# A graph network's first softmax stage: edge attributes loaded into the row buffers, gathers that add to them, and eight slots of rows in place of four

## What is computed

```python
h = jnp.maximum(_layernorm(x, axis=-1), 0.0)
# layer 0, per edge (src, dst) and per feature
m = jax.nn.relu(h[src] + edge_attr_64) + EPS
gmax = jax.ops.segment_max(m, dst, num_segments=N)
ex = jnp.exp(m - gmax[dst])
den = jax.ops.segment_sum(ex, dst, num_segments=N)
a = ex / den[dst]
msg = jax.ops.segment_sum(m * a, dst, num_segments=N)
...
# layer 1: mean of h[src] over dst; layer 2: a hyperbolic attention;
# layer 3: a relational attention with the same kind of softmax over dst
```

## Time and profile before

| | |
|---|---|
| Time, median of 3 runs | 9775.68 us (9775.22 to 9775.8) |
| Profiled execution, span from first to last instruction | 11897.1 us |
| PE busy | 6205.5 us (52%) |
| DVE busy | 7097.6 us (60%) |
| ACT busy | 4900.8 us (41%) |
| POOL busy | 7035.0 us (59%) |
| Gathers (indirect DMAs) of the four edge stages | 1664, 1664, 1840, 1664 |

### The profile page before, as it was taken

The page is one execution under the profiler, slowest core; times in us unless marked ns, Lnnn a source line. Parts: engine busy times, 40 slices in busy tenths (PEclk is TensorE's granted clock), DMA queues, the critical chain, the costliest instruction groups (busy, mean ns, idle before and its releaser), DMA issues. The chain is left out here.

```text
span 11897.1 us, 122808 instructions
## 1 busy us (share of the span) xinstructions
PE 6205.5 (52%) x28151; PEld 5446.9 (46%) x28151; DVE 7097.6 (60%) x14671; ACT 4900.8 (41%) x10378; POOL 7035.0 (59%) x7381
## 2 busy tenths in 40 slices
PE   3444444434255555551366666666665555555552
PEld 2444444432255555551356666666664344444441
DVE  5666666666455555531655555555555577777775
ACT  4555555532155555550244444444444222222221
POOL 5666666654666666667055555555554666666665
PEclk7667676665577777775555555555556666666665
DMA  5444444443222222222133444444444444444442
GB/s 117 112 111 111 111 110 110 110 89 130 55 56 57 56 56 56 57 55 20 32 78 79 81 81 80 80 82 80 80 81 135 106 116 115 115 116 113 116 114 78
DMA packets 1475564, 1051.26 MB, mean 88 GB/s; under 512 B 1027429, under 2 KB 1192798, under 8 KB 1474097
## 3 DMA queue, kind: packets, MB, share of 16 engines
q0 software_dynamic: 235520, 312.13, 14.7%
q1 hardware_dynamic: 842054, 371.05, 13.2%
q10 hardware_dynamic: 397557, 363.20, 9.4%
HBM read 574.49 MB, written 471.02 MB: 88 GB/s over the span
## 5 line engine op out<-in xcount | busy, mean ns | idle before, releaser
L1223 POOL DMA_INDIRECT h_rows_d<-table,h_idx_d x1840 | 1755.3, 954 | 1292.5 <-PE h_ps_sum L1243 698.0
L616 POOL DMA_INDIRECT rows<-table,idx_all x1664 | 1569.9, 943 | 974.7 <-issue 460.9
L1006 POOL DMA_INDIRECT m_rows<-table,idx_all x1664 | 1570.8, 944 | 877.4 <-issue 454.6
L616 POOL DMA_INDIRECT rows<-table3s,idx_all x1664 | 1570.0, 943 | 855.0 <-issue 475.8
L1036 PE MATMUL m_ps_sort<-m_hot_high,m_hot_low 128*128 128x224 f32 x3328 | 1050.4, 495 | 950.4 <-issue 793.0
L1036 PEld LDWEIGHTS m_ps_sort<-m_hot_high,m_hot_low 128*128 128x128 f32 x3328 | 916.0, 281 | 1056.0 <-issue 911.3
L1243 PE MATMUL h_ps_sum<-h_rows_d,h_hot 128*128 128x65 f32 x3680 | 831.3, 417 | 605.1 <-DVE h_rows_d L1380 354.6
L1243 PEld LDWEIGHTS h_ps_sum<-h_rows_d,h_hot 128*128 128x128 f32 x3680 | 794.8, 328 | 689.6 <-issue 689.6
L863 ACT ACTIVATE ex<-ex 128x512 f32<-128x512 f32 x416 | 261.9, 630 | 2010.3 <-issue 1060.6
L1261 PE MATMUL h_ps_src<-h_near,h_hot_t 128*128 128x65 f32 x3680 | 837.8, 419 | 405.9 <-DMA h_near<-table 218.0
L1261 PEld LDWEIGHTS h_ps_src<-h_near,h_hot_t 128*128 128x128 f32 x3680 | 804.1, 331 | 433.4 <-issue 432.5
(11 more groups left out here) (441 smaller groups left out, 15639.0 us busy)
## 6 DMA issues: line engine op xcount, KB each, us to landing
scan<-out_e ACTq DMA_DIRECT2D x832, 256.0 KB
h_near<-table SPq DMA_DIRECT2D x1840, 32.5 KB
run_g<-h_run ACTq DMA_DIRECT2D x230, 260.0 KB
part_b<-part SPq DMA_DIRECT2D x832, 64.0 KB
max_b<-top ACTq DMA_DIRECT2D x416, 128.0 KB
scan<-m_out_e SPq DMA_DIRECT2D x416, 128.0 KB
attr<-in_edge_attr SPq DMA_DIRECT2D x415, 128.0 KB
h_rows_d<-table,h_idx_d POOLq DMA_INDIRECT x1840
```

The source lines that it names most:

```text
L616: pool.indirect_dma_start(out=rows[:, b, k, h * GW:(h + 1) * GW], out_offset=None, in_=table3s.rearrange("n (q f) -> (n q) f", f=HEADS) if ...
L1006: pool.indirect_dma_start(out=rows[:, b, k, h * D:(h + 1) * D], out_offset=None, in_=table1, in_offset=bass.IndirectOffsetOnAxis(ap=idx_al ...
L1223: pool.indirect_dma_start(out=rows_d[:, b, k, :], out_offset=None, in_=table2, in_offset=bass.IndirectOffsetOnAxis(ap=idx_d[:, c * BT + k: ...
```

## The change

In the first stage the tile `attr` is gone. SP loads the edge attributes of a step straight into `rows`, where the gathered rows are to go, and the gathers carry `compute_op=ALU.add`, so that a gathered row is added to what lies in the buffer. `to_columns` is then one transpose for each of the four columns. `rows` has eight slots (`ROW_SLOTS`), each with semaphores `got_edge` and `got_rows` of its own. POOL no longer waits for the slot to be read but for the attributes of its step to have landed; SP waits for the slot (`turned` of step c-8). SP's order changes: at turn s it loads the attributes of step s, then `part_b` of step s-3. The fourth stage keeps four slots and plain gathers.

```diff
+ROW_SLOTS = 2 * SLOTS
...
-                rows = buf("rows", [P, SLOTS, TILES, HALVES * GW])
+                RS = SLOTS if rel else ROW_SLOTS
+                rows = buf("rows", [P, RS, TILES, HALVES * GW])
...
+                        def load_attr(c, b, r):
+                            slot_free(sp, rows_read, c, ago=RS)
+                            for h in range(HALVES):
+                                sp.dma_start(rows[:, c % RS, :, h * D:(h + 1) * D],
+                                             edge_rows(tail, 0) if c + h * STEPS == FULL else edge_rows(edge_attr, c + h * STEPS)) \
+                                    .then_inc(got_edge[c % RS], 16)
...
-                            else:
-                                slot_free(sp, rows_read, c, ago=SLOTS)
-                                last = isinstance(c, int) and c == STEPS - 1
-                                sp.dma_start(attr[:, b, :, 0:D], edge_rows(edge_attr, c)).then_inc(got_edge[b], 16)
-                                sp.dma_start(attr[:, b, :, D:2 * D], edge_rows(tail, 0) if last else
-                                             edge_rows(edge_attr, c + STEPS)).then_inc(got_edge[b], 16)
...
-                        written_out(STEPS, (1, load))
-                        if not rel:
+                        if rel:
+                            written_out(STEPS, (1, load))
+                        else:
+                            written_out(STEPS, (0, load_attr), (AHEAD, load))
...
-                            slot_free(pool, rows_read, c, ago=SLOTS)
+                            if rel:
+                                slot_free(pool, rows_read, c, ago=SLOTS)
+                            else:
+                                pool.wait_ge(got_edge[c % RS], c // RS * 32 + 32)
                             for k in range(TILES):
                                 for h in range(HALVES):
                                     pool.indirect_dma_start(
-                                        out=rows[:, b, k, h * GW:(h + 1) * GW], out_offset=None,
+                                        out=rows[:, c % RS, k, h * GW:(h + 1) * GW], out_offset=None,
                                         in_=table3s.rearrange("n (q f) -> (n q) f", f=HEADS) if rel else table0,
-                                        in_offset=bass.IndirectOffsetOnAxis(ap=idx_all[:, h, c, k:k + 1], axis=0)) \
-                                        .then_inc(got_rows[b], 16)
+                                        in_offset=bass.IndirectOffsetOnAxis(ap=idx_all[:, h, c, k:k + 1], axis=0),
+                                        compute_op=ALU.bypass if rel else ALU.add) \
+                                        .then_inc(got_rows[c % RS], 16)
...
                         def to_columns(c, b, r):
-                            pe.wait_ge(got_edge[b], r * 32 + 32)
                             slot_free(pe, weighed, c, ago=SCORES)
-                            pe.wait_ge(got_rows[b], r * ROWS + ROWS)
+                            pe.wait_ge(got_rows[c % RS], c // RS * ROWS + ROWS)
                             pe.sem_inc(pe_turn, 1)
                             for k in range(TILES):
-                                nc.tensor.matmul(ps_score[:, c % SCORES, k::TILES], rows[:, b, k, :], ident[:, :], start=True, stop=False)
-                                mm = nc.tensor.matmul(ps_score[:, c % SCORES, k::TILES], attr[:, b, k, :], ident[:, :],
-                                                      start=False, stop=True)
+                                mm = nc.tensor.transpose(ps_score[:, c % SCORES, k::TILES], rows[:, c % RS, k, :], ident[:, :])
                             mm.then_inc(turned, 1)
```

More of the change, by code:

```diff
@@ L492, in softmax_edges @@
                     own_v = buf("own_v", [HALVES * REL_HEADS, 2, W])
-                else:
-                    attr = buf("attr", [P, SLOTS, TILES, HALVES * D])
-                if rel:
                     score_c = buf("score_c", [P, W])
@@ L536, in softmax_edges @@
                     ps_v = psum("ps_v", [HALVES * REL_HEADS, W])
-                got_mask, got_edge, got_rows, put, put_top = ([sem(f"{n}{b}") for b in range(SLOTS)] for n in (
-                    "got_mask", "got_edge", "got_rows", "put", "put_top"))
+                got_mask, put, put_top = ([sem(f"{n}{b}") for b in range(SLOTS)] for n in ("got_mask", "put", "put_top"))
+                got_edge, got_rows = ([sem(f"{n}{b}") for b in range(RS)] for n in ("got_edge", "got_rows"))
                 seeded, v_turned, v_spread, v_kept, v_own, widened, turned, masked, moved, bent, carried, topped, lowered, diffed, exped, \
@@ L609, in _ @@
                         for c in range(STEPS):
-                            b = c % SLOTS
                             if not rel and c % (STEPS // IDX_PIECES) == 0 and c > 0:
                                 pool.wait_ge(got_idx[c // (STEPS // IDX_PIECES)], 16 * HALVES)
-                            slot_free(pool, rows_read, c, ago=SLOTS)
+                            if rel:
+                                slot_free(pool, rows_read, c, ago=SLOTS)
+                            else:
+                                pool.wait_ge(got_edge[c % RS], c // RS * 32 + 32)
                             for k in range(TILES):
```

## The result

| | before | after |
|---|---|---|
| Median | 9775.45 us (4 runs) | 10778.27 us (4 runs) |
| Range | 9771.44 to 9775.8 | 10775.86 to 10781.22 |

The change makes the kernel slower by 1002.8 us: ratio 1.1027, 95% interval 1.1014 to 1.1041. The measured time lies 218 us above the upper end of the stated range, 10560.

What follows compares the result with a forecast made beforehand. The prediction took POOL's issue of gathers to bound all four edge stages. It added 42 us for the adds and 3 us for the later start to 9775.7, giving 9821 us, with a range of 9690 to 10560.

Steps and rivals of the forecast that it cites:

- The bound: All four edge stages: POOL's issue of gathers sets the time, and in plain runs POOL hardly ever waits.
- the inference from two sums: Edge stages: POOL's waits, 2025.3 us, nearly match the profile's excess of 2121.4 us, so they belong to the profile.
- the faster rival: Gathers come faster than 1.228 us and slots remove 91 of 412 us of waits: 9688 us at best, chance 0.19.
- The ring: First stage: ACT and DVE take turns in 9.34 us a step, under POOL's 9.82 us of gathers.
- The terms at nothing: First stage: shorter transposes, eight slots and attribute loads each add 0, save about 3 us at the first gather.
- lower by 400 us or more: Sign expected in the changed profile: PE's busy time in the first stage falls by this much.
- Nearest row: the other kind of indirect DMA, a scatter ... I take 25 ns: First stage: an adding gather costs 25 ns more, as a scatter's 969 ns against 944, 42 us for 1664 gathers.
- The upper bound: First stage: an add's third place costs at most half of a gather's 944 ns, 472 ns each, 785 us in all.
- the row L2086: A gather with rows 32 times as long takes 954 ns, read as much of the instruction being a fixed cost.
- The rival with the two pages of the Trainium skill: First stage: POOL pays in full for an add's third descriptor, 785 us more, 10564 us, chance 0.20.
- The DMA engines: First stage: twice the gathers' 0.18 share leaves 0.72 used, hidden; adding rows would need 3.6 times as long to bound.
- The expected drop of the profiled span: Changed profile: the span may fall by some 100 us, with fewer PE instructions recorded, where plain runs gain nothing.

Runs made afterwards that it cites:

- e6: The kernel before, unedited, profiled once more: 9782.88 us, and its profiled span was that of a plain run.
- e4: The changed kernel with plain gathers and six of them a step, the last column's two left out: 9650.24 us, 141.3 below the kernel before.
- e1: The changed kernel with plain gathers in place of adding ones, all else as changed: 9792.89 us against 9791.55 for the kernel before, ratio 1.0001.
- e5: The changed kernel with a step's eight gathers in eight forms, adding and plain, of differing rows and row lengths: 10227.92 us against 9782.9 for the kernel before.
- e2: The changed kernel with adding gathers for one half of the edges, alternating with plain ones: 10322.44 us, ratio 1.0543 to the kernel before.
- e7: e2 with the four adding gathers of a step first and the four plain ones behind: 10311.7 us against 9794.37 for the kernel before, ratio 1.0528.

## Why the prediction was wrong

**The bound was right.** A plain run is one in which POOL hardly waits: e6 shows it without the inference from two sums. The interval of 1.248 us holds in plain runs too; the 1.228 that I got by assuming the node work as long as in the profile was some 2% low, and the 412 us of waits that the faster rival wanted to take away were not there.

**The ring was right.** 9.34 us; e4 measured the floor at 9.35, and a gain of 141 us where 133 had been worked out from it.

**The terms at nothing were right.** Transposes, slots, SP's order, attribute loads: e1 gives 1.3 us for all together, with an interval of about 10 us to each side, and in that the 3 us at the start (78.4 for 75.28) stand. e1 against e6, from 300 to 2100 us, columns as in the earlier trace rows, shows what PE gained. e6, the kernel before:

```profile
300.00:2100.00 1800.00, 1056.81 (x6149) 952.64 (x6148) 1432.85 (x1802) 1090.03 (x2522) 1360.60 (x1442) 0.72 0.51 132
```

And e1:

```profile
300.00:2100.00 1800.00, 729.48 (x3961) 585.58 (x3962) 1432.89 (x1801) 1089.98 (x2524) 1360.54 (x1442) 0.60 0.52 132
```

PE has 327 us less to do, DVE, ACT and POOL are the same to a tenth of a microsecond, and so is the time. The relief would have been over 327 had not the mean granted clock gone from 0.72 to 0.60 of full speed (its levels are 1.2 and 2.4 GHz), with PE idle for 1071 us of the stretch in place of 743: `to_rows`, which the change leaves alone, went from 319 to 406 ns a matmul. That is also why the sign "lower by 400 us or more" for PE did not come: 1170 us in the stage before, 831 in the changed kernel's stage.

**The step that failed is "Nearest row: the other kind of indirect DMA, a scatter ... I take 25 ns".** The term was 42 us and measured 1000. The path was the right one, POOL's issue with no cover, and the price on it was off by a factor of 24: 25 ns more a gather were taken, and 601 measured. The prediction's own sign of being wrong, a gather longer by over 200 ns, came. Three things went wrong. The scatter is near in name only: it adds nothing to what lies at its destination, so it says nothing on what an add costs. The upper bound was no bound. "Were all of the 944 ns spent on these, one more costs half of it" supposes that an add does the same work as a copy, once more by half; e5 shows some 425 ns that an add pays whatever the number of rows, beside a cost by rows that more than doubles. And the row L2086 was asked for more than it says. It has 98 rows of 2080 floats for 128 of 64, so it shows that bytes don't count, as e5 confirms; it says little on the cost of a row. That most of a plain gather is fixed came out right in e5 (some 840 of 944 ns) and not from that row, and a large fixed part of the known instruction says nothing on the fixed part of an unknown one. It argued for neither end, and I let it argue for the low one.

**The rival with the two pages of the Trainium skill** ("Collectives: The Full Stack", the bandwidth ceiling; "DMA: Bandwidth & Descriptors", SWDGE vs HWDGE vs iDMA) had the right direction, and a price of 785 us that was too small by 215. That the direction was right does not show its mechanism. By the rule of a third descriptor the part by rows should grow by half; in e5 it more than doubles, and the larger, fixed part isn't in the rule. The traces thus agree that an add is dearer to issue and don't agree with the price of half more. What POOL does in the extra time no trace here shows, so why the add costs what it costs stays open.

**The DMA engines** had room. The gathers' queue took 20.5% of the stretch from 300 to 3000 us in the changed kernel:

```profile
q0 software_dynamic: 210096, 47.90, 20.5%
```

For e6, from 300 to 2100 us:

```profile
q0 software_dynamic: 46166, 47.36, 14.0%
```

For one gather that is 0.205 x 2700 / 1460 = 0.38 us of all 16 engines, for 0.14 x 1800 / 1442 = 0.17 before: 2.2 times as much for the same bytes, where twice was assumed and 3.6 times would have been needed to bound the stage. The prediction's 0.18 for this queue in a plain run was too high, since it carried the share of the whole span over to the first stage, where 0.14 was measured. The total share of the engines was 0.51 in e6 (0.54 had been worked out) and 0.47 in the longer stage of the changed kernel.

**The expected drop of the profiled span** by fewer PE instructions had no ground: e6's span shows that before had no such excess of its own.

## What to carry to other kernels

Where one engine issues without a pause, ask first what the change does to the length of each instruction that it issues; work taken from any other engine is worth nothing there, here 327 us of PE's. Moving an addition into an indirect DMA is no free ride on bytes that move anyway: the engine that issues it pays, 601 ns a gather here, mostly per instruction and not per row. When the trace has no row of a form on the bounding engine, a change of form has no upper bound from rows of other forms: the range must be open on that side, and the first measurement is that one instruction's duration.

## What the runs showed that was not expected

- A profiled execution can have thousands of microseconds of waits that plain runs of the same kernel lack: 11897.1 us once and 9781.1 the next time, with the gathers of each edge stage as long to within 5 us of busy time. A sum over the waits against the plain median told it apart.
- An adding gather moves in many more packets: the queue has 421888 for 235520 before, with the same 312.13 MB. That is 112 more for each of 1664 gathers, 144 for 32 (210096 / 1460, 46166 / 1442), which fits one packet for each row of 256 bytes where a plain gather puts eight rows in one.
- The issue of an indirect DMA depends on the kind of the ones ahead of it: a plain gather right behind adding ones is 35 to 55 ns longer, an adding one behind four plain ones 35 to 47, and this dies away over two or three. Why is open; it was seen in e2, e5 and e7 alone.
